# Relation picks written to PSUM, and 31 instead of 28 tiles gathered in the second neighbour sum of a graph kernel

## What is computed

```python
def _layer(h, nbrs, Wr, Wi, br, bi, tr, ti, ebr, ebi):
    h = _crelu(h @ W.T + b)
    w = _evolution_row(deg, tr, ti)
    out = w[0] * h
    for k in range(deg):
        out = out + w[1 + k] * h[nbrs[:, k]]
    return out + (ebr + 1j * ebi).astype(jnp.complex64)
...
h = _layer(h, nbrs, W1r, W1i, b1r, b1i, t1r, t1i, eb1r, eb1i)
h = _layer(h, nbrs, W2r, W2i, b2r, b2i, t2r, t2i, eb2r, eb2i)
return h.real
```

```python
a = hs @ Ws.T + h[dst] @ Wd.T + emb_rel[etype] @ Wr.T
e = jax.nn.leaky_relu((a @ attn_fc2_w.T)[:, 0], 0.01)
```

## Time and profile before

| | us |
|---|---|
| timed runs, median of 3 (lowest to highest) | 9962.77 (9959.43 to 9967.66) |
| span of the profiled execution | 9952.3 |
| all instructions, per cent of the span: PE 78, PEld 61, DVE 80, ACT 60, POOL 70 | |

### The profile page before, as it was taken

One profiled execution on the slowest core, in us unless ns is written; L12 is line 12 of the kernel. 1 busy time (PEld: TensorE's weight loads), 2 busy tenths in 40 slices (PEclk: granted clock), 3 DMA queues, 4 the chain that ended last, 5 costly groups with the idle time before them and its releaser, 6 DMA issues.

```text
span 9952.3 us, 178573 instructions
## 1 busy us (share of the span) xinstructions
PE 7715.9 (78%) x39865; PEld 6093.7 (61%) x39865; DVE 7995.6 (80%) x24833; ACT 5948.5 (60%) x18344; POOL 6964.8 (70%) x7476
## 2 busy tenths in 40 slices
PE   4444444554799998998898999888888888848887
PEld 3333444444477777777677777666666666636665
DVE  7776666666888887999867778788888888899999
ACT  6777777777977773111100016688888888846665
POOL 0377777777188887777678876566666666649994
PEclk6555555556899999999899999855565555557776
DMA  2322222222688888877766652322222222210000
GB/s 52 52 53 54 52 53 53 53 52 59 219 242 242 239 236 270 288 286 284 249 239 224 229 203 61 80 50 49 50 50 49 50 49 50 49 27 1 1 1 27
DMA packets 530134, 1151.52 MB, mean 116 GB/s; under 512 B 147135, under 2 KB 398211, under 8 KB 508751
## 3 DMA queue, kind: packets, MB, share of 16 engines
q0 software_dynamic: 241872, 477.23, 20.3%
q10 hardware_dynamic: 22752, 517.02, 13.2%
q1 hardware_dynamic: 264478, 145.85, 5.6%
HBM read 886.72 MB, written 259.31 MB: 115 GB/s over the span
## 4 chain that ended last, share of the span: by engine, by line
DVE 24%; PE 23%; POOL 22%; issue 13%; ACT 12%; DVEq 2%; DMA 2%; SPq 1%; ACTq 0%; POOLq 0%
POOL onehot L2198 10%; PE bank L1426 8%; POOL step_data L1756 7%; ACT bank_tile L1188 3%; POOL step_data L1462 3%; PE bank_tile L2055 3%; DVE keys L1484 2%; DVE keys L1112 2%; PE bank L1052 2%; ACT onehot L1041 2%; DVE keys L1121 2%; POOL gather_ring L1462 2%; ACT onehot L1039 2%; PE bank_tile L2065 2%; DVE keys L2035 2%
## 5 line engine op out<-in xcount | busy, mean ns | idle before, releaser
L1027 POOL DMA_INDIRECT gather_ring<-mean_rows,step_data x1660 | 1596.7, 962 | 745.9 <-issue 324.8
L1052 PE MATMUL bank<-gather_ring,onehot 128*128 128x130 f32 x3320 | 946.2, 449 | 1131.9 <-DVE arena L1085 960.8
L1426 PE MATMUL bank<-arena 128*128 128x384 bf16 x8526 | 1639.1, 332 | 29.6 <-DMA arena<-split_out 26.4
L1426 PE MATMUL bank<-arena,keys 128*128 128x384 bf16 x8526 | 1627.1, 331 | 10.9 <-DMA arena<-split_im 10.9
L1052 PEld LDWEIGHTS bank<-gather_ring,onehot 128*128 128x128 f32 x3320 | 793.7, 301 | 1278.4 <-issue 1048.7
L1426 PEld LDWEIGHTS bank<-arena 128*128 128x128 bf16 x8526 | 1180.7, 139 | 297.8 <-issue 58.8
L1426 PEld LDWEIGHTS bank<-arena,keys 128*128 128x128 bf16 x8526 | 1178.9, 139 | 272.2 <-issue 36.9
L1756 POOL DMA_INDIRECT step_data<-next_rows,window_idx x896 | 1045.2, 1167 | 349.4 <-issue 264.0
L1462 POOL DMA_INDIRECT step_data<-hidden,window_idx x888 | 1064.6, 1199 | 297.7 <-issue 264.0
L1979 POOL DMA_INDIRECT gather_ring<-attention_rows,step_data x834 | 786.6, 943 | 436.1 <-PE bank_tile L2055 224.4
L1979 POOL DMA_INDIRECT keys<-attention_rows,step_data x826 | 779.5, 944 | 384.8 <-PE bank_tile L2055 223.4
(11 more groups left out here) (350 smaller groups left out, 20262.2 us busy)
## 6 DMA issues: line engine op xcount, KB each, us to landing
keys<-count_rows ACTq DMA_DIRECT2D x50, 3136.0 KB
arena<-count_rows ACTq DMA_DIRECT2D x50, 3136.0 KB
count_rows<-arena ACTq DMA_DIRECT2D x26, 3136.0 KB
count_rows<-keys ACTq DMA_DIRECT2D x26, 3136.0 KB
gather_ring<-mean_rows,step_data POOLq DMA_INDIRECT x1660
step_data<-next_rows,window_idx POOLq DMA_INDIRECT x896
step_data<-hidden,window_idx POOLq DMA_INDIRECT x888
gather_ring<-attention_rows,step_data POOLq DMA_INDIRECT x834
```

The lines of the kernel that those rows point to most:

```text
L1027: e.indirect_dma_start(ring_at(rings.slot(name, i), SUM_COLS, SUMS - 1), None, rows, bass.IndirectOffsetOnAxis(src_idx[:, i:i + 1], 0), bo ...
L1052: e.matmul(pass_bank[i % N_SUM_BANKS][:, 0:SUMS], onehot[:, i % STEP_SLOTS, :], ring_at(rings.slot(name, i), SUM_COLS, SUMS), start=True, ...
L1426: m = e.matmul(pass_bank[n % 2][:, 0:SPLIT_COLS], counts[t % 2][:, :, h], split[:, h, :], start=(h == 0), stop=(h == NODE_TILES - 1))
```

## The change

`picked` is laid over banks 2 to 5 of PSUM, which are `count_bank`, instead of over words of `window_idx`. For that the eight banks are now one tensor (`banks`) instead of five; their places stay. The wait before the first pick asks that the last of the first round's count tables has been copied out of these banks (`counted`), where it asked for the products and the digits. The built tables of the second sum still start behind the last pick, as before. And `SECOND` goes from 28 to 31: 67 dense tiles and 31 gathered ones, 15 tables built instead of 18.

```diff
--- before.py
+++ after.py
@@ -37,6 +37,7 @@
 LOAD_PARTS = 125
 LOAD_COLS = EDGES // LOAD_PARTS
 
+BANKS, BANK_WORDS = 8, 512
 PIECES = 3
 AW = 132
 A_DEN, A_NMAX, A_SDST = D, D + 1, D + 2
@@ -72,7 +73,7 @@
 DENSE = 52
 FOLDED = 23
 GATHERED = NODE_TILES - DENSE
-SECOND = 28
+SECOND = 31
 DENSE2 = NODE_TILES - SECOND
 BUILT = DENSE2 - DENSE
 ROUND = DENSE * GROUPS
@@ -336,9 +337,10 @@
     signs = sb("signs", [P, 7])
     first_row = sb("first_row", [P, D])
 
-    pass_bank = [stack.enter_context(nc.psum_tensor(f"bank{i}", [P, 512], F32)) for i in range(4)]
-    tile_banks = stack.enter_context(nc.psum_tensor("bank_tile", [P, LANE // 2], F32))
-    tile_bank = [tile_banks[:, i * 512:(i + 1) * 512] for i in range(4)]
+    banks = stack.enter_context(nc.psum_tensor("banks", [P, BANKS * BANK_WORDS], F32))
+    pass_bank = [banks[:, i * BANK_WORDS:(i + 1) * BANK_WORDS] for i in range(4)]
+    tile_banks = banks[:, 4 * BANK_WORDS:]
+    tile_bank = [tile_banks[:, i * BANK_WORDS:(i + 1) * BANK_WORDS] for i in range(4)]
     bank_all = pass_bank + tile_bank
 
     def table(name, width):
@@ -406,7 +408,7 @@
     rest_many = keys[1][:, TILE_SLOTS * SPLIT_COLS:].rearrange("p (s c) -> p s c", c=2 * D)
     score_all = inv_deg
     edge_score = keys[0][:, 0:STEPS]
-    picked = window_idx[:, DEG * GATHERED:DEG * GATHERED + STEPS].bitcast(F32)
+    picked = banks[:, 2 * BANK_WORDS:2 * BANK_WORDS + STEPS]
     edge_coef, edge_norm = edge_score, window_idx[:, 0:STEPS].bitcast(F32)
     count_bank = [pass_bank[2], pass_bank[3], tile_bank[0], tile_bank[1]]
     end_bank = [tile_bank[2], tile_bank[3]]
@@ -1718,8 +1720,7 @@
             e.wait_ge(n.sem, n.n)
             return e
 
-        e.wait_ge(built, ROUND)
-        e.wait_ge(digit_steps, DIGITS * DENSE)
+        e.wait_ge(counted, ROUND)
         own().memset(edge_score, 0.0).then_inc(n.sem, n.up())
         for r in range(RELATIONS):
             own().tensor_scalar(picked, edge_type[:, 0:STEPS], float(r), rel_score[:, r:r + 1], ALU.is_equal,
```

## The result

| | kernel before | changed kernel |
|---|---|---|
| timed runs on the same chip, median of 11 each (lowest to highest) | 9966.65 us (9959.43 to 9972.88) | 9943.26 us (9934.95 to 9951.52) |
| ratio to the kernel before, 95% interval | | 0.9976 [0.9968, 0.9983] |
| span of the profiled execution | 9952.3 us | 9932.5 us |

The changed kernel is faster by 23 us (0.24%), 20 us by the two profiled spans. The forecast was 76 us faster by the spans, 9887 us, in a range of 9840 to 9947. The direction was right, the range held the time by 4 us, and the size was missed by two thirds.

A forecast was written before the change was run, and what follows sets the result against it. GpSimd's stalled gathers bound the second sum while picks run, the tensor engine its rest, the vector engine the round before. 108 us gained less 32 lost is 76, giving 9887 us, range 9840 to 9947.

The forecast's parts named there:

- The stall of 1.5 us for each pick pair: Second neighbour sum, while picks run: pick and addition stop GpSimd's gathers, 1.5 us lost per pair; picks in PSUM end this.
- rival 4: Gathers still stalled 1.5 us per pair despite picks in PSUM; second sum ends 59 us late, kernel 10054 us; chance 0.04.
- The pick's price, 0.78 us: Vector engine: a pick written to PSUM takes 1.88 us instead of 1.10, 0.78 us more for each.
- The new wait: Before the first pick: waiting for the copies of the first round's counts, not only their products, costs nothing.
- The second round, 32 us longer: Second round of the first neighbour sum: 72 longer picks add 56 us of vector work, 12 to 56 us longer, 32 taken.
- The early part, 57 us shorter: Second neighbour sum while it has picks: with gathers unstalled it ends at 5850 instead of 5907 us.
- 20 us for what they wait for each other: Second sum while picks run: allowance because three engines within 15 us of each other cannot all be full.
- rival 1: Vector engine's idle time while picks run only halves, from fixed order; 919 us there, kernel 9963, no change; chance 0.14.
- The late part, 51 us shorter: Second neighbour sum after the picks: 390 fewer tensor instructions save 64 us, 13 lost to GpSimd; 407 us instead of 458.
- GpSimd's debt of 13 us: Second sum after the picks: GpSimd arrives without a lead, needs 407 us where the tensor engine needs 394.
- Rival 3: The pick keeps its speed in PSUM, so the first sum's second round costs nothing; kernel 9850 us; chance 0.07.
- Rival 2: Vector engine's idle time while picks run all stays, longer picks add whole; 123 us slower, kernel 10086; chance 0.06.

The follow-up runs named there:

- the later ends: Changed kernel with the second sum's transpose, product and last copies at each tile's end 4 slots later: 9881.25 us, ratio 0.9925 to the kernel before.

## Why the prediction was right or wrong

**The stall of 1.5 us for each pick pair, and that it goes: right.** 944 ns instead of 1266 for a gather beside the picks, 0.945 was taken. Both instructions of the pair stalled by themselves. In the early part before, 68 of the 74 gathers that began under a pick ended 0.8 us after that pick, and 111 of the 125 that began under an addition ended 0.8 us after that addition; now 392 gathers begin under either of them, and none takes over 0.96 us. That the pick into PSUM is harmless to gathers, taken without a row for it, held too. With the picks in SBUF and 31 tiles the early part is 1034 us, where rival 4's sum had 6017 - 4991 = 1026. The Trainium skill, "GPSIMD Engine Reference", section "Specifications", says that vector instructions in a two-port mode or with two SBUF inputs contend with GpSimd; the new pair has neither, and the old pair one of each, if it was a two-port mode that gave the pick its 0.67 ns a column, where the addition takes 1.03. The traces agree with both halves of it.

**The pick's price, 0.78 us: nearly right.** It is 0.84 (1.94 us instead of 1.10). The Trainium skill, "VectorE: DVE Perf Modes", section "Why PSUM operands drop a tier", was the warning, and here it holds for an operand that is written; the estimate of 1.85 us from the page's cycle table was 5% short. The addition stayed (1883 ns beside 1888).

**The new wait: right.** The memset ahead of the picks has 0.3 us of idle time as before.

**The second round, 32 us longer: mis-sized, inside its ends.** It is 51 us longer. 72 picks by 0.84 are 60 us more vector work (56 were taken), and 85% of it came through, not 57%. (The longer of the two ends, 1130 us, is 60 us more than 1070 and not 56.) The step that failed is the middle value, taken between a vector engine 97% busy and one 93% busy: it is 94% busy by the stretch up to 5013 us (1050 of 1120). Waits for the tensor engine did not shrink with a later vector engine; the tensor engine's own wait for a row grew by 45 us instead. With the pick shortened by half or by one instruction, the round falls by 127 and 111 us for 123 and 132 us less vector work, so at this load the round follows the vector engine nearly one for one.

**The early part, 57 us shorter: the step that failed.** It is 10 us shorter. Each engine's own need was right: the tensor engine was given 834 us and is busy 829.6, the vector engine 792 and is busy 790, GpSimd's gathers came in time. (At the 93% of the round, 853 us, the vector engine would have ended at 5844 and not at 5838, which changes little.) What was wrong is "I add 20 us for what they wait for each other". The tensor engine waited 75.8 us. The row for it was in front of me: 80.0 us of waiting for L1225. I put the stretch's idle time down to the gathers as a whole, and rival 1 names the fixed order. But rival 1 halves the vector engine's idle time for no stated mechanism. The mechanism is the distance of 8 slots between a tile's beginning and its transpose, 24.5 products or some 4 to 5 us of tensor work, into which the norm chain of 2 us, a pick pair and at times a batch sum must fit. With a pair of 3.0 us the waits that follow on no late gather come to 17 us; with one of 3.8 to 58 us at 28 tiles, and at 31, with closer batches, to 76. In numbers rival 1 was nearer: it gave the vector engine 127 us of idle time and the early part 919 us, measured 116 and 906, and the kernel 9963 us, 20 from the measured 9943, where the forecast is 56 away. That this is the cause, and not only a tale that fits, is shown by the later ends: 849 us with the same instructions, ten less than the 859 that I had forecast from restart to last pick, and the same shift gives nothing in the kernel before.

**The late part, 51 us shorter: right by its mechanism, its debt not due.** It is 60 us shorter. The tensor engine's part (64) came. GpSimd's debt of 13 us rested on an early part of 859 us, in which it would have no lead. In one of 906 it had time for a lead of two batches (704 gathers, 688 due), and the debt was paid there. Where the early part is 846 to 857 us the late part is 402 to 409, as forecast (407), and the debt is seen in it: with the later ends the vector engine waits 40.5 us for gathers there, in the changed kernel 13.0.

**The sum**: 51 lost, 10 and 60 gained, 19 in the profile; forecast 32 lost, 57 and 51 gained. That the time still lies in the range is thin, by 4 us, and owed to the 9 us more of the late part. The long early part accounts for 47 of the missing 57 us, the round for 19, and the late part gave 9 back.

**The rivals.** Rival 3 (cheap pick) and rival 4 (gathers still stalled) are out by their rows. Rival 2 (the idle time kept, the pick added whole) was to turn the change into a loss from 119 us of idle time of the vector engine upward; 116 are there. That point was worked out with 56 us lost in the round and 51 gained in the late part. With rival 2's own late part of 394 us it lies at 132. Measured are 51 and 60, so 19 us are left of a gain that I had put at 76.

## What to carry to other kernels

An idle time that two causes can share doesn't go when one of them goes: ask, for each engine that waits in a fixed order, what stands on the other engine between a value's being ready and its being written, and how long that is after the change. When an instruction grows, list what is queued behind it for another engine; a few slots more between the request and the value can cost nothing and be worth more than the change. And two edits that are worth nothing or less by themselves can pay together when one makes the room that the other fills, so such a pair is to be measured as four kernels. When the waits of one order are gone, look at what is full next: with shorter picks and with later ends it was GpSimd, and on top of the later ends the shorter pick took nothing more off the early part (850 us beside 849).

## What the runs showed of the hardware that was not expected

- A vector instruction of 1660 columns that writes to PSUM takes 1942 ns with one SBUF bf16 input, one that reads PSUM and SBUF and writes SBUF 1883, and one that multiplies and adds in one step (L1734) 1944: two operations for the price of one, here with one input in PSUM.
- A gather that begins under a vector instruction that stalls it ends 0.8 us after that instruction (179 of 199 in the early part before; the 199 take 1.17 to 3.02 us instead of 0.94).
- The tensor engine's instructions, nearly all of them dense products, read 2% shorter where it stands less: 811.8 us for 4981 instructions with the later ends, 829.6 for 4990 without, at a granted clock of 0.99 and 0.98, and 856.0 for 4968 at 0.91 with the 31 tiles alone.
- Two chips ran every kernel that was put on them about 10% longer than the others, and an edit that is worth +8 to +11 us elsewhere cost 184 and 233 us there. A verdict of some tenths of a per cent should not be carried from one such chip to another.
